# A graph attention layer on one core: queries by one matmul of 192 columns, and fewer table rows fetched by SyncE

## The reference

```python
src, dst = edge_index
q = (X @ Wq)[src]                  # 64 wide
k = (X @ Wk)[dst]                  # 64 wide
e = jnp.tanh(q + k)
scores = e @ Wphi
scores = scores - jnp.max(scores)
exp_scores = jnp.exp(scores)
denom = jax.ops.segment_sum(exp_scores, src, num_segments=N)
alpha = exp_scores / (denom[src] + 1e-09)
vy = (X @ Wy_w + Wy_b)[dst]
ve = e @ We
out = jax.ops.segment_sum(alpha[:, None] * (vy + ve), src, num_segments=N)
# and: layernorm(x + out)
```

## Time and profile before

| | us |
|---|---|
| median of 3 runs | 7010.81 |
| lowest, highest | 7007.23, 7012.87 |
| the profiled execution, its own time | 7016.36 |
| its span, first to last instruction | 7014.5 |
| main loop, first gather to the end of the last | 1315.99 to 6901.09 |
| DVE idle before L1154 | 1335.6 |
| POOL idle before L1085 | 2496.0 |

### The profile page before, as it was taken

One profiled execution on the slowest core, in us unless ns is written; L12 is line 12 of the kernel. 1 busy time (PEld: TensorE's weight loads), 2 busy tenths in 40 slices (PEclk: granted clock), 3 DMA queues, 4 the chain that ended last, 5 costly groups with the idle time before them and its releaser, 6 DMA issues. The chain is left out here.

```text
span 7014.5 us, 115608 instructions
## 1 busy us (share of the span) xinstructions
PE 3898.3 (56%) x25925; PEld 2946.3 (42%) x25925; DVE 3592.0 (51%) x8202; ACT 2751.7 (39%) x10900; POOL 3447.3 (49%) x3516
## 2 busy tenths in 40 slices
PE   7899999554544544544444445445445444454456
PEld 6555555343433433433434334334334334343346
DVE  7788888544444444444444444444444444444446
ACT  3788888322322322323223223223223223232235
POOL 1133323455655555655555555555555555555552
PEclk9766666666666666666666666666666666666668
DMA  2100000222322222222222222222222222222234
GB/s 82 45 4 4 5 4 4 62 75 75 84 74 77 80 75 81 80 74 79 77 76 81 76 75 84 74 78 80 79 80 77 75 79 79 75 82 76 76 91 100
DMA packets 288906, 479.68 MB, mean 68 GB/s; under 512 B 96903, under 2 KB 208745, under 8 KB 287988
## 3 DMA queue, kind: packets, MB, share of 16 engines
q0 software_dynamic: 164032, 321.94, 17.4%
q1 hardware_dynamic: 106418, 145.33, 6.5%
q10 hardware_dynamic: 17794, 4.91, 0.3%
HBM read 456.45 MB, written 20.60 MB: 68 GB/s over the span
## 5 line engine op out<-in xcount | busy, mean ns | idle before, releaser
L1085 POOL DMA_INDIRECT gathered<-table,dst_rows x3252 | 3109.2, 956 | 2496.0 <-PE bank L1120 1167.3
L1120 PE MATMUL bank<-gathered,weighted_onehots 128*128 128x193 f32 x6592 | 1939.8, 437 | 997.1 <-issue 677.5
L1120 PEld LDWEIGHTS bank<-gathered,weighted_onehots 128*128 128x128 f32 x6592 | 1519.4, 257 | 1145.2 <-issue 901.7
L1109 PE MATMUL bank<-q_parts,src_onehots_T 128*128 x9888 | 818.0, 215 | 1996.7 <-DVE src_onehots_T L1154 1460.1
L1129 ACT ACTIVATE gathered<-gathered 128x256 f32<-128x256 f32 x824 | 346.3, 420 | 3597.9 <-DVE gathered L1168 3305.6
L1109 PEld LDWEIGHTS bank<-q_parts,src_onehots_T 128*128 128x128 bf16 x9888 | 686.3, 108 | 2271.3 <-issue 2160.6
L1192 DVE TENSOR_TENSOR block_sums<-block_sums,bank 128x193 f32 x3296 | 1169.2, 355 | 637.5 <-issue 198.9
L1140 ACT ACTIVATE weighted_onehots<-src_onehots,edge_weight 128x128 f32<-128x128 bf16 x3296 | 1075.3, 397 | 26.9
L817 ACT ACTIVATE places_past_far<-bank,stat 128x98 bf16<-128x98 f32 x2727 | 884.7, 400 | 129.3 <-DVE place_col L800 58.1
L1168 DVE TENSOR_TENSOR gathered<-bank,gathered 128x256 f32<-128x256 f32 x824 | 345.8, 420 | 1145.3 <-remote 1124.2
L1154 DVE TENSOR_SCALAR src_onehots_T<-src_in_block_rows,partition_number_from 128x2048 bf16<-128x2048 bf16 x206 | 155.2, 754 | 1335.6 <-DMA src_in_block_rows<-src_in_block_list 1280.5
(11 more groups left out here) (182 smaller groups left out, 2021.7 us busy)
## 6 DMA issues: line engine op xcount, KB each, us to landing
src_in_block_rows<-src_in_block_list SPq DMA_DIRECT2D x206, 512.0 KB
gathered<-table SPq DMA_DIRECT2D x5632, 0.8 KB
gathered<-table,dst_rows POOLq DMA_INDIRECT x3252
table<-in_x SPq DMA_DIRECT2D x4, 1562.5 KB
x_in<-in_x SPq DMA_DIRECT2D x24, 256.0 KB, 3.0
x_again<-in_x SPq DMA_DIRECT2D x48, 128.0 KB, 2.3
out<-out_rows SPq DMA_DIRECT2D x48, 128.0 KB, 1.9
sorted_list<-sorted_groups,unit_destinations POOLq DMA_INDIRECT x248
```

The source lines that it names most:

```text
L1085: e.indirect_dma_start(slot[:, r, j, 0:ROW], None, table, bass.IndirectOffsetOnAxis(ap=gidx[:, t:t + 1].bitcast(u32), axis=0)).then_inc(ga ...
L1109: made = e.matmul(QK[q % 2][:, j * A:(j + 1) * A], ohT[:, c % 2, o:o + PARTS], q3[:, bass.ds(b + s_ * A, A)], start=s_ == 0, stop=s_ == 2)
L1120: made = e.matmul(SM[q % 2 * 2 + j // 2][:, o:o + SUMS], ohw[:, q % 3, j, :], slot[:, r, j, A:SLOT], start=True, stop=True)
```

## The change

Three things are changed, all in the main loop.

The three parts of a tile's queries are no longer summed by PE. One matmul of 192 columns for each tile writes the three parts side by side; two tiles fill 384 columns of a bank, so a step takes two banks, and `QK` are two pairs of banks. DVE sums the parts by two reductions, each over two tiles, from PSUM into the slot, reading the three values of a sum 64 elements apart. A new semaphore, `query_summed`, lets the addition of the keys wait for them; the addition now reads both of its inputs from the slot in SBUF.

`PERIOD` becomes 144 steps (36 chunks), with which `NSP` becomes 5: SP fetches the rows of 5 steps, POOL those of 819.

SP's share for each chunk becomes 16 rows in place of 32, in chunks 2 to 33 of the period.

```diff
-        PERIOD = 18 * QUADS_PER_CHUNK
+        PERIOD = 36 * QUADS_PER_CHUNK
...
+        query_summed = sem("query_summed")
...
-        QK, SM = [bank[0], bank[1]], [bank[4], bank[5], bank[6], bank[7]]
+        QK, SM = [[bank[0], bank[1]], [bank[2], bank[3]]], [bank[4], bank[5], bank[6], bank[7]]
...
-                    share = 2 * CHUNK
+                    share = CHUNK
...
-                        for s_ in range(3):
-                            made = e.matmul(QK[q % 2][:, j * A:(j + 1) * A], ohT[:, c % 2, o:o + PARTS], q3[:, bass.ds(b + s_ * A, A)],
-                                            start=s_ == 0, stop=s_ == 2)
+                        made = e.matmul(QK[q % 2][j // 2][:, j % 2 * 3 * A:(j % 2 + 1) * 3 * A], ohT[:, c % 2, o:o + PARTS], q3[:, bass.ds(b, 3 * A)],
+                                        start=True, stop=True)
...
-                    e.tensor_tensor(slot[:, r, :, ROW:ROW + A], QK[q % 2][:, 0:QUAD * A].rearrange("p (j f) -> p j f", f=A), slot[:, r, :, 0:A],
-                                    ALU.add).then_inc(added_qk, 1)
+                    for h in range(2):
+                        made = e.tensor_reduce(slot[:, r, 2 * h:2 * h + 2, ROW:ROW + A], QK[q % 2][h][:, 0:6 * A].rearrange("p (j s f) -> p j f s", s=3, f=A),
+                                               AX.X, ALU.add)
+                    made.then_inc(query_summed, 1)
+                    e.wait_ge(query_summed, q + 1)
+                    e.tensor_tensor(slot[:, r, :, ROW:ROW + A], slot[:, r, :, ROW:ROW + A], slot[:, r, :, 0:A], ALU.add).then_inc(added_qk, 1)
```

More of the change, by code:

```diff
@@ L993, in gnn_program @@
         leave = {k: sem(f"pass_next_{k}") for k in ENGINES if k != "sync"}
-        pass_sems = [*gathered, *rows_by_sync, *lows_loaded, sums_cleared_vector, onehots_made, onehots_T_made, queried, added_qk, tanh_made,
+        pass_sems = [*gathered, *rows_by_sync, *lows_loaded, sums_cleared_vector, onehots_made, onehots_T_made, query_summed, queried, added_qk, tanh_made,
                      times_phi, scored, weights_made, weighted, totalled, accumulated, row_max, core_max, shift_made, eps_made, *steps_over.values()]
-        QK, SM = [bank[0], bank[1]], [bank[4], bank[5], bank[6], bank[7]]
+        QK, SM = [[bank[0], bank[1]], [bank[2], bank[3]]], [bank[4], bank[5], bank[6], bank[7]]
         H3 = NB * SUMS // 3
```

## The result

| | before, us | changed, us |
|---|---|---|
| median of 4 runs | 7009.02 (6986.53 to 7012.87) | 6223.87 (6221.82 to 6227.96) |
| profiled execution, own time | 7016.36 | 6224.39 |
| its span | 7014.5 | 6222.6 |

The ratio is 0.8886, with a 95% interval of 0.8867 to 0.8906: 11% faster, 36 us from the forecast. The chip of these runs is called W here. On X, Y and Z the kernel before takes 5547 to 5549 us, and on Y, where the changed kernel ran again as it is, it is 3% *slower*. So the forecast held for W; why it did, and what it missed, is what the experiments tell.

The account below looks back on a forecast made before the run. SP's late issue of rows was taken to bound the loop; 814 steps at 5.88 us for 5547.6 us give -762, +11 at the ends, so 6265, and 6260 us for the median; range 6200 to 6340 us (0.56).

Parts of the forecast that it names:

- SP's queue is the bound: Main loop: SP issues table rows in order, 28 to 29 us of work per chunk, and every engine follows it.
- SP's work for 16 rows: SP's queue after the change: 19 to 23 us per chunk, against 23.5 us of POOL, so SP stops being last.
- The floor of 5.88 us a step: POOL's gathers with their pauses: what the loop falls to when SP is lightened, 814 x 5.88 = 4786 us.
- at the ends: Five steps at either end of the loop: DVE's longer chain, 1.1 us a step, shows only there, +11 us.
- rival (e): POOL's pauses shrink with PE's and SP's work: a step goes to 5.0 us, 5545 us in all; chance 0.09.
- DVE's cover: DVE's idle time before L1168, 9.6 us per chunk, hides the 4.4 us that the reductions add per chunk.
- rival a, b: DVE's reductions not hidden: 1.1 us on each step, about 7145 us, chance 0.08; half of it, 6420 to 6630 us, 0.16.
- rival d: DVE's addition, now with two SBUF inputs, blocks POOL's gathers: at most 344 us more, 6604 us; chance 0.05.
- PE at nothing: PE's query matmuls, twelve of 64 columns becoming four of 192 per step: gain costed at nothing.
- rival c: SP's queue stays last at 25.5 us a chunk in place of 23.5: +320 us, 6580 us; chance 0.06.

Follow-up runs that it names:

- slowed kernels: Kernel before and changed kernel, each with SP loading its 16 registers again ahead of every third table row: 6956.55 and 5730.2 us, beside 5547.39 for the kernel before.
- the halves: Comparison L1157 split into two of half size; on V, with SP's part alone 6348.14 us (0.8901), in the kernel before 7013.22 (0.9828).

## Why the prediction was right, and where only by its chip

- **SP's queue is the bound**, 28.86 us a chunk: right for W. The slowed kernels on Z show that such a queue is enough to give this time, and V that SP's part takes 9.5% away. That the rows were dear for a reason of the chip could not be seen in one trace; that they were dear only beside POOL's gathers could, and the prediction read it.
- **SP's work for 16 rows, 19 to 23 us:** 19.50 + 1.7 = 21.2 us on W. SP waited before L1061 for DVE for 184.3 us in 38 of some 150 chunks, so it has stopped being last, with little to spare. On Y the same wait is 2345.8 us.
- **The floor of 5.88 us a step:** 5.83 on W. It carried the sum: -801 us for the -762 of the forecast. The 9 us at the ends for 11 are in part luck, since 3.5 of them lie before the first gather. But the floor is no property of POOL's gathers. On X a step takes 5.03 us (SP's part alone), the number of rival (e), 1.25 x 4 = 5.0, though not by its cause: on Y the kernel before has no such pauses either, with all its work for PE and SP. On such a chip the prediction's own sum would have said: nothing to gain, 30 us to lose by six steps.
- **DVE's cover (rival a, b):** it held on W as far as the time tells; more reductions were run on X only. One reduction more on X gave no more time than the changed kernel on Y; the second, which brought DVE's chunk to 22.25 us, cost 373 us. The cover ends where the prediction had it, when DVE's chunk passes POOL's, only that POOL's is 20.4 us on X and not 23.5.
- **The addition blocks POOL (rival d):** the step that failed. "The trace doesn't show it blocking" was read from L1176 at 6746.18 beside a gather begun at 6745.92. That gather had started 0.26 us *ahead* of L1176, and what counts is 0.125 us after its start. The row above it showed the mechanism: the gather at 6744.33 began within L1154 (6744.05 to 6744.80) and ended at 6745.62, 0.82 us behind its end. The price was set by L1157 and L1154 more than by the addition: of 172.1 us of loss on W (before: 3109.2 - 3252 x 0.945 = 36.1) they take 71.2 and 49.4, the addition 27.5 and L1180 16.9, against the 344 of rival (d). The forecast came through this unharmed because the floor had most of it in: in the two stretches from which the 5.88 was read, 49 gathers lost 1.9 and 2.4 us, 0.16 to 0.20 us a step, and after the change it is 172.1 / 819 = 0.21. That was luck, as the prediction put the loss at nothing. On Y, where the kernel before loses 0.04 us a step, it decides the sign.
- **PE at nothing:** right as far as the sum goes. PE's busy time from 2000 to 5000 us falls from 2070.37 to 1742.74 us on Y and no time follows. Whether it gives something on W was not run apart.
- **SP stays the bound (rival c):** not so. On W the last 26 chunks, without SP rows, take 23.0 us, those with rows 23.3.

## What to carry to other kernels

Before costing an engine's queue by its durations, see whether each instruction there is dear by itself or dear in company; if it is the second, the gain hangs on that condition, and the result of one chip isn't that of the next. A cover in time isn't one in ports: beside a POOL that gathers without pause, look for the DVE instructions that are running 0.1 us after a gather starts, and keep them short or off that moment. A new instruction can cost more by shifting the others than by itself. SP's fewer rows are the robust half of this change: 9.5% on V (with the halves), and 0.4% slower on X, where the queries' part alone costs 148 us.

## What the runs showed of the hardware that I had not expected

- Two kinds of chip for one program: 7009 and 7131 us on W and V, 5547 to 5549 on X, Y and Z, at the same durations of all single instructions of the loop but L1154. On W SP starts a row every 1.2 us or so beside POOL's gathers and every 0.4 to 0.5 us without them (means of the kernel before, register loads included), on Y every 0.46 to 0.48 beside them. PE is late as well: from 2000 to 5000 us it stood 617 us in 410 gaps that end on nothing the profile shows, on Y 0.6 us in 4; for DVE the two chips are alike, 149 and 144 us. POOL mostly stops after 8 gathers (after 12 or 16 in the changed kernel), for 2.2 us in the median. What makes a chip one or the other, whether it is the chip at all or something else that was common to its runs, and what ties POOL's stops to 8, stays open.
- A gather's wait for a DVE instruction ends 0.82 us ahead of the gather's end to within 0.01 us, for L1154, L1157, L1173 and L1180 alike, and costs 0.97 us in the longest shown (1.91 for 0.945).
- More DVE work can make the kernel faster: one reduction that nobody needs brought the loss from 184.4 us (Y) to 90.9 (X).
